# Image 0 summed in six banks side by side, images 1 and 2 in another order, another order in the preparation and at the end

## The reference

```python
perceived = conv_general_dilated(x, w_perc, padding='SAME', feature_group_count=C) + b_perc
hid = gelu(einsum('bphw,dp->bdhw', perceived, w_up1) + b_up1, approximate=False)
x_new = x + einsum('bdhw,cd->bchw', hid, w_up2) + b_up2
...
scores = stack([(q * kp[:, 1+dy:1+dy+H, 1+dx:1+dx+W, :]).sum(-1) for dy, dx in _POS], -1) * scale
out = sum(softmax(scores)[..., i:i+1] * vp[shifted by _POS[i]] for i in range(9))
return h_new + out
```

## Time and profile before

| | us |
|---|---|
| median of 3 runs | 400.92 (400.87 to 401.61) |
| the profiled execution | 401.61 |
| its span, first to last instruction | 399.8 |
| PE busy | 385.9 |
| DVE busy | 339.9 |
| ACT busy | 320.4 |
| POOL busy | 174.5 |

### The profile page before, as it was taken

How to read it: one execution, slowest core, us unless ns; L and a number is a source line. 1 busy time by engine, 2 the same in 40 slices (tenths; PEclk the granted TensorE clock), 3 DMA queues, 4 the chain that set the end, 5 groups by cost and what they waited for, 6 DMA issues and landing times.

```text
span 399.8 us, 10521 instructions
## 1 busy us (share of the span) xinstructions
PE 385.9 (97%) x3680; PEld 362.4 (91%) x3680; DVE 339.9 (85%) x922; ACT 320.4 (80%) x713; POOL 174.5 (44%) x154
## 2 busy tenths in 40 slices
PE   6999798999999999999999999999999999999994
PEld 4999697999999999999999999999999999999784
DVE  5999989888878988888888988888898888886875
ACT  6544579889797979979797988979797997978882
POOL 6737263635425263543516363552526354230110
PEclk9999999999999999999999999999999999999996
DMA  7320302004050220405031130504022030301003
GB/s 245 156 68 2 119 2 89 33 0 174 2 167 8 71 102 0 171 0 171 0 123 48 30 140 0 171 0 167 4 61 110 0 105 2 107 0 54 3 28 131
DMA packets 11513, 28.58 MB, mean 71 GB/s; under 512 B 2400, under 2 KB 3296, under 8 KB 11488
## 3 DMA queue, kind: packets, MB, share of 16 engines
q1 hardware_dynamic: 10640, 28.20, 20.6%
q10 hardware_dynamic: 848, 0.05, 0.1%
HBM read 19.86 MB, written 8.39 MB: 71 GB/s over the span
## 4 chain that ended last, share of the span: by engine, by line
PE 78%; DVE 11%; ACT 4%; issue 3%; POOL 1%; ACTq 1%; DVEq 0%; POOLq 0%
PE m_ps L464 43%; PE s_ps L542 9%; PE work L474 9%; PE work L516 6%; PE s_ps L525 5%; DVE t L855 3%; PE s_ps L508 2%; PE s_ps L511 2%; PE s_ps L509 2%; ACT pt L724 1%; DVE ab L847 1%; PE m_ps L542 1%; ACT L684 1%; DVE s_ps L897 1%; POOL hid_lo L1197 1%
## 5 line engine op out<-in xcount | busy, mean ns | idle before, releaser
L464 PE MATMUL m_ps<-thi,whi 128*128 128x248 f32 (+1 forms) x576 | 163.9, 285 | 0.6 <-DVE y L968 0.5
L464 PE MATMUL m_ps<-thi,wlo 128*128 128x248 f32 (+1 forms) x576 | 160.5, 279 | 0.0
L464 PE MATMUL m_ps<-tlo,whi 128*128 128x248 f32 (+1 forms) x576 | 159.2, 276 | 0.0
L464 PEld LDWEIGHTS m_ps<-thi,whi 128*128 128x128 f32 x576 | 108.2, 188 | 3.8 <-DVE y L968 0.7
L464 PEld LDWEIGHTS m_ps<-tlo,whi 128*128 128x128 f32 x576 | 109.0, 189 | 0.6
L464 PEld LDWEIGHTS m_ps<-thi,wlo 128*128 128x128 f32 x576 | 108.2, 188 | 0.0
L1197 POOL TENSOR_TENSOR hid_lo<-hid,hid_hi 128x1024 fp32r<-128x1024 f32 x30 | 72.5, 2415 | 22.3 <-ACT hid_hi L674 21.1
L724 ACT COPY pt<-ptc 32x256 f32<-32x256 f32 (+3 forms) x189 | 74.3, 393 | 5.0 <-DVE ptc L1021 0.4
L1174 POOL TENSOR_TENSOR fc<-xp 128x512 f32<-128x512 f32 x16 | 21.4, 1334 | 111.3 <-DVE tlo L862 109.3
L664 ACT ACTIVATE hid<-y,b1eff 128x1024 f32<-128x1024 f32 x31 | 35.7, 1151 | 37.4 <-DVE y L968 22.9
L738 ACT ACTIVATE p_sb<-p_sb,negmax 128x101 f32<-128x101 f32 x128 | 46.8, 369 | 7.3 <-DVE negmax L1002 7.2
(11 more groups left out here) (139 smaller groups left out, 775.8 us busy)
## 6 DMA issues: line engine op xcount, KB each, us to landing
xp<-x_planes SPq DMA_DIRECT2D x16, 640.0 KB, 5.5
xr<-x_rows SPq DMA_DIRECT2D x16, 512.0 KB, 4.1
out<-o_sb SPq DMA_DIRECT2D x28, 256.0 KB, 4.1
out<-y SPq DMA_DIRECT2D x3, 256.0 KB, 2.2
w1T<-w SPq DMA_DIRECT2D x1, 384.0 KB, 3.1
out<-y SPq DMA_DIRECT2D x2, 128.0 KB, 1.9
w2T<-w SPq DMA_DIRECT2D x1, 128.0 KB, 4.4
wqk_in<-w_qk SPq DMA_DIRECT2D x1, 128.0 KB, 4.4
```

The source lines that it names most:

```text
L464: last = pe.matmul(m_ps[:, b, col + first:col + end], a[:, j, dy, half * P:(half + 1) * P], c[:, par, T_PLACE[j], first + by:end + by], st ...
```

## The change

- **Preparation.** The loads of `bp`, `b1`, `b2` move from ACT's queue to SP's. The first load of gelu's table no longer waits for `w1T`. Plane 5's high and low weights come second instead of last but one. `w2lo` and `wqk_lo` move from DVE to POOL. Five `keep_busy` go, four warm-up matmuls with `warm_done` come.
- **Image 0.** Its two halves are summed in six banks, `m_ps` 0 and 1 and `s_ps` 0 for half 0, `work` 2, `m_ps` 2 and `s_ps` 1 for half 1, plane by plane (1, 5, 3, 2, 4, 0), each for both halves. The twelve `between_units` go.
- **Images 0 to 2.** The bodies are rewritten on all engines, as below.
- **The end.** Copies of `place(0, 2)` move from ACT to DVE, all zero keys and maxima of the last image come ahead of the second and third `take_v`, image 14's two additions become one, and eight matmuls into a bank that nobody reads are added between the last `values`.

```diff
@@ PE
+        def m_bank(n, half, b):
+            if is_image(n, 0):
+                return ((m_ps[:, 0, :], m_ps[:, 1, :], s_ps[:, 0, :]),
+                        (work[:, 2, :], m_ps[:, 2, :], s_ps[:, 1, :]))[half][b]
+            return m_ps[:, b, :]
...
-                keep_busy(5)
                 pe.matmul(work[:, 2, 2 * P + 2:2 * P + 3], bq_wide[:, :], bqk[:, 1:2], start=True,
                           stop=True).then_inc(wt_ready, 1)
+                for _ in range(4):
+                    last = pe.matmul(m_ps[:, 2, S:CH], w1T[:, 0, 0:P], w1T[:, 0, 0:S], start=True, stop=True)
+                last.then_inc(warm_done, 1)
...
+            def first_image():
...
+                products(0, 0, 0, 1)
...
+                products(0, 0, 0, 5)
...
+                products(0, 0, 1, 1)
+                products(0, 0, 1, 5)
+                for j, k in ((3, 3), (2, 4), (4, 5)):
+                    pe.wait_ge(wlo_dve_done, k)
+                    for half in range(2):
+                        last = products(0, 0, half, j)
...
+                for half in range(2):
+                    products(0, 0, half, 0).then_inc(m_ready, 1)
...
-                units(0)
-                between_units(12)
-                units(1, 4, 2, 3)
...
+                units(4, 5)
+                if is_image(n, 1):
+                    units(6, 7, 8)
+                    up(n)
+                    units(9, 10, 11)
                 else:
-                    units(4, 5)
-                if attn:
-                    up(n)
-                units(6, 7, 8)
+                    if attn:
+                        up(n)
+                    units(6, 7, 8)
...
-                for g in range(2):
-                    pe.wait_ge(pt_done, (n - 2) * PLACED + 15 + 6 * g)
-                    pe.wait_ge(pt_dve_done, 9 + 6 * g)
+                for g, fillers in enumerate((5, 3)):
+                    for _ in range(fillers):
+                        pe.matmul(s_ps[:, 0, 0:S], whi[:, M_ORDER[0], 0, 0:P], thi[:, 0, 0, :], start=True, stop=True)
+                    pe.wait_ge(pt_done, (n - 2) * PLACED + 12 + 6 * g)
+                    pe.wait_ge(pt_dve_done, 12 + 6 * g)
                     values(n + 2, 1, g)
@@ ACT
+                if is_image(n, 0):
+                    take_m13(0, 0)
+                    high_t(1, 1)
+                    take_m13(0, 1)
+                    gelu(0, 0)
+                    high_hid(0, 0)
+                    prime_gelu()
+                    return
+                if is_image(n, 1):
+                    take_m13(1, 0)
+                    gelu(0, 1)
+                    high_hid(0, 1)
+                    take_m13(1, 1)
+                    for c in range(NCH):
+                        high_h(1, 0, c)
+                    for c in range(NCH):
+                        take_q(1, c)
+                    high_t(2, 0)
+                    gelu(1, 0)
+                    high_hid(1, 0)
+                    gelu(1, 1)
+                    for i in range(T):
+                        exp(1, i)
+                    prime_gelu()
+                    return
+                if is_image(n, 2):
+                    high_hid(1, 1)
+                    take_m13(2, 0)
+                    place_p(2, 0, (0, 1, 2))
+                    for c in range(NCH):
+                        high_h(2, 1, c)
+                    place_p(2, 0, (3,))
...
@@ DVE
+                if is_image(n, 0):
+                    transform_ab(1, 1)
+                    transform(1, 1)
+                    combine(0, 0)
+                    low_t(1, 1)
+                    combine_y(0, 0)
+                    finish_y(0, 0)
+                    combine(0, 1)
+                    combine_y(0, 1)
+                    finish_y(0, 1)
+                    return
+                if is_image(n, 1):
+                    combine(1, 0)
+                    combine_y(1, 0)
+                    transform_ab(2, 0)
+                    finish_y(1, 0)
+                    sum_h(1, 1)
+                    low_h(1, 0)
+                    transform(2, 0)
+                    combine(1, 1)
+                    low_t(2, 0)
+                    combine_y(1, 1)
+                    finish_y(1, 1)
+                    softmax_front(1, 1)
+                    for g in range(2):
+                        sums(1, g)
+                        turn_p(1, g)
+                    return
+                if is_image(n, 2):
+                    transform_ab(3, 1)
+                    combine(2, 0)
+                    sum_h(2, 0)
+                    low_h(2, 1)
+                    transform(3, 1)
+                    combine_y(2, 0)
+                    finish_y(2, 0)
+                    low_t(3, 1)
+                    softmax_front(2, 0)
...
@@ DVE, last
                 take_v(n, hp, 0)
-                add_zero_keys(n, 0)
-                row_max(n, hp, 0, 1)
-                add_zero_keys(n, 1)
+                place(0, 2)
+                for g in range(2):
+                    add_zero_keys(n, g)
+                    row_max(n, hp, g, None)
                 sums(n, 0)
-                row_max(n, hp, 1, 2)
+                take_v(n, hp, 1)
+                add_h(n, 1, 1)
+                take_v(n, hp, 2)
+                sums(n, 1)
                 turn_p(n, 0)
...
@@ POOL
+                if is_image(n, 0):
+                    sums_ab(1)
+                    differences(2, 0)
+                    pool.wait_ge(y_part_done, 8)
+                    low_hid(0, 0)
+                    return
+                if is_image(n, 1):
+                    low_hid(0, 1)
+                    sums_ab(2)
+                else:
+                    if more:
+                        sums_ab(n + 1)
+                    if attn:
+                        low_hid(n - 1, 1)
                 if conv and (not isinstance(n, int) or n + 2 < B):
                     pool.wait_ge(tlo_done, n * 2 + 4)
                     differences(n + 2, par)
```

More of the change, by code:

```diff
@@ L436, in small_weights, with products @@
                 pe.wait_ge(bq_wide_done, 1)
-                keep_busy(5)
                 pe.matmul(work[:, 2, 2 * P + 2:2 * P + 3], bq_wide[:, :], bqk[:, 1:2], start=True,
                           stop=True).then_inc(wt_ready, 1)
+                for _ in range(4):
+                    last = pe.matmul(m_ps[:, 2, S:CH], w1T[:, 0, 0:P], w1T[:, 0, 0:S], start=True, stop=True)
+                last.then_inc(warm_done, 1)
+            def products(n, par, half, j):
+                b, col = M_PLACE[j]
+                bank = m_bank(n, half, b)
+                steps = [(dy, a, c) for dy in (1, 0, 2) for a, c in ((whi, thi), (whi, tlo), (wlo, thi))]
+                for s, (dy, a, c) in enumerate(steps):
+                    first, end = max(0, (1 - dy) * WIN), min(S, S + (1 - dy) * WIN)
+                    by = (dy - 1) * WIN
+                    last = pe.matmul(bank[:, col + first:col + end], a[:, j, dy, half * P:(half + 1) * P],
+                                     c[:, par, T_PLACE[j], first + by:end + by], start=(s == 0),
+                                     stop=(s == len(steps) - 1), skip_group_check=True)
+                return last
             def unit(n, par, i):
@@ L459, in unit @@
[L459 to L466, removed]
+                last = products(n, par, half, j)
@@ L630, in body @@
                         score(n, 1 - par, g)
-                units(9, 10, 11)
+                if not is_image(n, 1):
+                    units(9, 10, 11)
             steady(pe, body, last_attention)
@@ L816, in body @@
                 if attn:
-                    for i in range(4):
-                        exp(n, i)
-                if attn:
-                    for i in range(4, T):
+                    for i in range(T):
                         exp(n, i)
@@ L998, in row_max @@
                 dve.wait_ge(z_done, n * 4 + (2 * g - 2))
-                take_v(n, hp, part)
+                if part is not None:
+                    take_v(n, hp, part)
                 for u in range(4):
@@ L1128, in body @@
                 if attn:
[L1129 to L1132 removed]
+                    softmax_front(n, par)
                     sums(n, 0)
```

176 lines of the change are left out of this document (103 added, 73 removed).

## The result

The changed kernel takes 405.49 us (median of 4 runs, 405.40 to 405.83); the kernel before took 401.13 beside it (400.87 to 401.61). The ratio is 1.0112 (95% interval 1.0100 to 1.0124): **4.4 us slower**, where 401.8 was forecast with a range of 397.6 to 403.4. The sign was right, the size was not, and the time lies outside the range.

The account below looks back on a forecast made before the run. TensorE, busy 385.9 of 399.8 us, was taken as the bound. Start and image 0 -2.6, image 1 to `up` of image 2 +5.1, behind it -1.4, clock +1.6, end -1.8: +0.9 on the median 400.92, so 401.8 us, range 397.6 to 403.4.

Parts of the forecast that it names:

- Start and image 0: Up to image 1's first unit: first unit near 15.95, image 0 in six banks without gaps; 2.6 us gained.
- Image 1 and the hole: Image 1 to `up` of image 2: two PE waits of 3.9 and 3.0 us there, `up` ending 2.5 us later.
- the wait before unit 4 of image 1: PE waits 0.85 us for VectorE's second `combine` of image 0.
- t: Moment when the second half of y of image 1 is finished: forecast 54.8, before 58.7.
- the high part: ACT's high part of the hidden layer, at t+7.9; PE waits 3.9 us for it in `up` of image 2.
- the low part: POOL's low part of the hidden layer, at t+11.8; PE waits 3.0 us for it in `up` of image 2.
- Behind it: After `up` of image 2: the 0.98 wait at the queries and 0.4 of smaller ones go; 1.4 us gained.
- +1.6 for the clock: PE's clock falls in the waits of `up` of image 2, costing 1.6 us, bounds 0 and 3.1.
- the piece at 73.80: Stretch of PE's profile before the change in which image 3 starts, one third of the way in, at 76.9.
- Images 3 to 15 run the same program after the change, so they move as a block.: Only image 3's start and what follows image 15 were taken to count.
- The end: After image 15: earlier copies, and eight fillers holding the clock through the last ten matmuls; 1.8 us gained, bounds 0.2 and 2.3.
- the clock falls at the end as well: Rival, between the two last sets of matmuls: PE stands too long, price 1.6 us, total 403.4; chance 0.12.

Follow-up runs that it names:

- e2: The changed kernel with 28 and 18 filler matmuls ahead of TensorE's two waits in `up` of image 2: 402.61 us.
- e4: The changed kernel with POOL's differences of image 3 held back until VectorE's four operations for image 1's second half of y are done: 402.92 us.
- e8: The changed kernel without the two stores of image 14, which is missing from its output: 404.60 us.
- e9: e5 with eleven fillers in `up` of image 3, POOL's `low_hid(2, 0)` behind VectorE's y, and the end's fillers cut to 5 and 0: 398.65 us.
- e11: The kernel before with only the three bias loads on SP's queue and the early gelu table load: 400.78 us against 400.91.
- e1: The changed kernel with both parts of image 1's second-half hidden layer made straight behind its gelu, ahead of exponentials and normalisations: 401.94 us.
- e3: The changed kernel with ACT making the high part of image 3's planes ahead of image 2's two query copies: 403.48 us.
- e6: The kernel before with only the change's new end, including its eight filler matmuls: 400.61 us against 400.97.
- e7: The changed kernel without the end's eight filler matmuls: 405.02 us.
- e10: e6 without the last three of its eight filler matmuls: 400.54 us.
- e5: The changed kernel with the orders of images 1 and 2 written anew on ACT, VectorE and POOL: 398.95 us, ratio 0.9945 to the kernel before.

## Why the prediction was wrong, step by step

*Start and image 0, forecast -2.6, was -2.0.* The twelve units run without a gap, 1.04 apart, and no weight is late behind the first. What was off is the first unit: 16.43 for 15.95. VectorE's first accumulation came 0.25 earlier as forecast, but in this profile the unit stands behind PE's own warm-up and small products, and these take longer or shorter from one execution to the next: ten take 4.04 in the profile before, 4.50 in that of after, between 3.76 and 4.50 in the others, whatever the preparation. Where they were through sooner (e2, e4, e8, e9, the same start), the unit waited 0.18 to 0.65 for VectorE's low weights and began at 16.05 to 16.66, so 15.95 came out in none. e11 shows that the moved loads and the early table load bring nothing.

*Image 1 and the hole, forecast +2.5 at the end of `up` of image 2.* Right in every step but one size (the wait before unit 4 of image 1 was 0.45, not 0.85): t 54.4 (54.8), the high part ready at 62.4 (62.7), the wait 3.73 (3.9), the low part at 66.3 (66.6), the wait 2.66 (3.0); `up` ends at 67.5 (67.2). e1 and e4 show both halves of the cause, the order behind t and the meeting of VectorE and POOL.

*Behind it, forecast -1.4 and +1.6 for the clock.* Image 3 started 3.06 late, 78.0+1.6 = 79.6 against 80.02 measured. The clock cost 2.0 instead of 1.6 (e2). The mechanism was right, the size was taken from the one slow stretch seen, which was too short. It isn't one size either: in e8, whose front is the same, the slow stretch of the profiled execution (mean clock 0.987) reaches to 73 and images 2 and 3 take 59.24, 0.74 more; two of the changed kernel's four runs have that mean clock, the profiled one has 0.990. (A slip without effect: 27 of 63 matmuls are not a third of the piece at 73.80 but 3.1 of its 7.49 us; the 76.9 worked out from them is right.)

*"Images 3 to 15 run the same program after the change, so they move as a block."* **This step failed, at a cost of 1.3 us.** Images 3 to 15 do run the same program, but image 3 begins with VectorE and ACT where image 2 left them, and the new order of image 2 leaves them late against PE: ACT's `high_t(3, 1)` behind `take_q`, VectorE's wait of 2.02 for it. The prediction followed only PE's own start into image 3. e3 undoes that one order and gets 1.2 back.

*The end, forecast -1.8.* **This term was mis-sized, at a cost of some 1.4 us.** It was read from the profiled execution of before (401.61 us, clock 0.51 in the last ten matmuls) and added to the median (400.92). In the runs that make the median the clock most likely doesn't fall there: e11, with the same gaps, has 1.68 us for them, and only nine of 48 runs have the mean clock of the profiled one. (No run of the kernel before at its median was profiled.) The prediction noted that the profiled run was 0.7 above the median and used a term that holds what makes that run slow. Of the 1.8 some 0.56 are real up to the last addition (e11 against e6), and the transfers behind it leave 0.36 (e6). The rival "the clock falls at the end as well" hung on the same misreading: neither the fillers (e7, e10) nor these gaps decide it.

*What no step had:* the time outside the span, 1.8 in every run of the kernel before, was 1.80 to 2.85, on average 2.2, in the four runs of the changed one.

Sum of the misses against 401.8: first unit, hole and clock 0.4, image 3 1.3, end 1.4, outside the span 0.4: 3.5 of 3.7.

## What to carry to other kernels

When a change rewrites the stages ahead of a steady loop, note for every engine, not only for the bound one, where it stands against that one at the seam, before and after: the loop's first pass pays for whichever is behind. Before a term is taken from a profile, see whether the profiled execution has the median's time and clock, since a stretch that makes this one run slow is no gain to be had from the median. Put what the bound engine waits for ahead of work whose result is wanted later: such orders alone were worth the 6.5 us between the changed kernel and e5.

## What the runs showed of the hardware

The granted clock doesn't follow from the longest gap. It fell behind gaps of 0.37 and 1.24 us with about 1 us of matmuls between them (e5), and held through one of 1.32 (e7); with gaps of 1.31 and 0.55 it fell in the profile before and held in that of e11. One program meets both, as far as mean clocks tell: of the 48 runs of the kernel before nine have 0.991 or 0.992, like its profile, and 39 at least 0.996; of e5's four runs one has 0.994, the others 0.997 or 0.998; of e1's ten six have 0.993 or 0.994, four 1.000.

The time outside the span was 1.74 to 1.91 us in all runs of the kernels whose clock falls nowhere ahead of the end (before, e2, e6, e9, e10, e11), and 1.74 to 3.65 in those whose profile has it fall inside images 2 or 3 (changed, e1, e3, e4, e5, e7, e8). Run by run the two do not go together: the four runs of e1 with a mean clock of 1.000 have 2.13 to 3.51, the run of e8 with the lowest mean clock, 0.987, has 1.79. What happens in that time no trace shows, and it stays open.
